# Sorted edge rows kept by step, lane and slot, and a second attention loop that loads them directly

## What is computed

```python
def _L2_gnn_ref(x, edge_attr, Wq, bq, Wk, bk, Wv, bv, We, be, bias, edge_index):
    H, C = 8, 32
    q = (x @ Wq + bq).reshape(n, H, C)
    k = (x @ Wk + bk).reshape(n, H, C)
    v = (x @ Wv + bv).reshape(n, H, C)
    dst = edge_index[0]
    src = edge_index[1]
    e = (edge_attr @ We + be).reshape(-1, H, C)
    key_j = k[src] + e
    alpha = (q[dst] * key_j).sum(-1) / math.sqrt(C)
    alpha = jax.nn.softmax(alpha, axis=0)
    out = v[src] * alpha[:, :, None]
    out = jax.ops.segment_sum(out, dst, num_segments=n)
    return out.reshape(n, H * C) + bias
# for each layer L of the four:
    h = jnp.maximum(_layernorm(x, axis=-1), 0.0)
    x = x + L(h, edge_index, ...)
```

## Time and profile before

| | |
|---|---|
| median of 3 runs | 4075.86 us (4073.83 to 4079.36) |
| span of the profiled execution | 4069.4 us |
| busy | PE 2803.7 (69%), DVE 2921.2 (72%), POOL 2699.3 (66%), ACT 942.5 (23%) |
| first attention loop, first to last step | 1675 to 2283 us |
| second attention loop, first to last step | 2519 to 3257 us |

### The profile page before, as it was taken

One profiled execution on the slowest core, in us unless ns is written; L12 is line 12 of the kernel. 1 busy time (PEld: TensorE's weight loads), 2 busy tenths in 40 slices (PEclk: granted clock), 3 DMA queues, 4 the chain that ended last, 5 costly groups with the idle time before them and its releaser, 6 DMA issues. The chain is left out here.

```text
span 4069.4 us, 59078 instructions
## 1 busy us (share of the span) xinstructions
PE 2803.7 (69%) x13465; PEld 1627.6 (40%) x13465; DVE 2921.2 (72%) x6759; ACT 942.5 (23%) x2732; POOL 2699.3 (66%) x2789
## 2 busy tenths in 40 slices
PE   5436779999997999699999876888888840000007
PEld 4335322222223887355555443555555530000004
DVE  7897458888885333599999774777777775666664
ACT  0020112222221332344444321222222220000004
POOL 0486667777664777677777475777777727777772
PEclk8555889999998999799999898999999975555558
DMA  4477357777765333577777433666666614444440
GB/s 173 151 237 269 88 156 208 205 202 201 206 195 134 63 68 70 157 211 212 211 208 207 100 83 102 191 191 189 191 190 191 186 40 109 108 108 108 108 105 33
DMA packets 418425, 627.24 MB, mean 154 GB/s; under 512 B 254045, under 2 KB 275650, under 8 KB 417296
## 3 DMA queue, kind: packets, MB, share of 16 engines
q0 software_dynamic: 173536, 520.88, 45.2%
q1 hardware_dynamic: 236336, 76.88, 8.0%
q10 hardware_dynamic: 8448, 28.18, 2.1%
HBM read 548.80 MB, written 76.56 MB: 154 GB/s over the span
## 5 line engine op out<-in xcount | busy, mean ns | idle before, releaser
L1219 POOL DMA_INDIRECT edge_ring<-tab,edge_rec x480 | 469.3, 978 | 199.7 <-issue 128.1
L2204 POOL DMA_INDIRECT state<-tab,edge_rec x480 | 453.9, 946 | 158.0 <-issue 145.9
L1843 PE MATMUL edge_psS<-edge_terms,ident 128*128 128x256 f32 x1952 | 471.5, 385 | 34.6 <-DVE edge_psS L1887 34.6
L1843 PEld LDWEIGHTS edge_psS<-edge_terms,ident 128*128 128x128 f32 x1952 | 369.1, 193 | 203.7 <-DVE edge_psS L1887 107.9
L2376 PE MATMUL gate_psT<-ident,gate_hb 128*128 128x128 f32 x50 | 10.0, 287 | 614.7 <-ACT gate_hb L2337 614.7
L1763 POOL DMA_INDIRECT state<-tab,edge_rec x360 | 340.4, 946 | 127.6 <-issue 104.5
L1281 PE MATMUL edge_psX<-state,ident 128*128 x720 | 377.7, 634 | 53.6 <-DVE edge_ring L1310 53.3
L1763 POOL DMA_INDIRECT state<-tab,edge_feat x360 | 340.4, 946 | 109.7 <-issue 104.8
L1862 PE MATMUL edge_psX<-state,ident 128*128 128x512 f32 x720 | 351.9, 612 | 84.5 <-DMA state<-tab,edge_feat 82.0
L1310 DVE TENSOR_TENSOR edge_ring<-edge_psX,edge_ring 128x1024 f32<-128x1024 f32 x240 | 293.9, 1225 | 97.2 <-PE edge_psX L1290 49.3
L1882 DVE TENSOR_TENSOR edge_terms<-state,edge_psW 128x1024 f32<-128x1024 f32 x180 | 219.8, 1221 | 116.9 <-ACT edge_psW L1820 110.5
(11 more groups left out here) (471 smaller groups left out, 6116.9 us busy)
## 6 DMA issues: line engine op xcount, KB each, us to landing
feat_d<-state SPq DMA_DIRECT2D x32, 528.0 KB, 5.1
sorted_d<-state SPq DMA_DIRECT2D x7, 2380.0 KB
edge_feat<-feat_d SPq DMA_DIRECT2D x113, 132.0 KB
state<-tab,edge_rec POOLq DMA_INDIRECT x840
state<-src_rows ACTq DMA_DIRECT2D x26, 512.0 KB
state<-low_rows ACTq DMA_DIRECT2D x26, 512.0 KB
edge_ring<-tab,edge_rec POOLq DMA_INDIRECT x600, 3.7
update_row_out<-in_edge_all SPq DMA_DIRECT2D x57, 128.0 KB
```

What stands on the lines that cost most here:

```text
L1219: pool.indirect_dma_start(out=ring[:, k, s, :], out_offset=None, in_=S["tab0"][:, :], in_offset=bass.IndirectOffsetOnAxis(ap=rec[:, k, R_S ...
L1843: last = pe.matmul(so_far, S["ident"][:, :], terms[:, s, :], start=False, stop=(s == QE - 1), skip_group_check=True)
L2204: pool.indirect_dma_start(out=ring[:, k, s, :], out_offset=None, in_=S["tab3"][:, :], in_offset=bass.IndirectOffsetOnAxis(ap=rec[:, k, R_S ...
```

## The change

Rows of `sorted_d` now lie by step (512 rows), within a step by lane, within a lane by slot, as long as there are at most NEAR_STEPS = 128 steps (`many` = 0 on the chip; with more steps `many` = 1, the rows lie as before and every step is gathered). So the rows of step k, all lanes, are one block of 512 rows, and SP can load it with one direct transfer.

- **attend(2):** SP's loop of near turns loads for each step the record and then the rows (`load_near`); POOL's loop has only the 4 gathers, which wait for `s_feat`. The last turn is a loop of its own: SP loads a record and then waits until POOL's gather of that step has landed (`pass_on`) before it goes to the next; POOL gathers three steps' rows first, then alternates. Near turns are all turns but one.
- **rank_edges:** the steps of the second order are prepared before the table `before` is made, since the place of a node now depends on the step at which its block begins (`apart`, `begins`, one more matmul); `before` counts in units of 128 rows, and a third matmul for each column of each look-up adds the lane (`lane_b`). The place is then taken apart into step, lane and slot (9 more instructions on 128 x 416), and the record turn has 3 more.
- **order_nodes:** the blank is 8 transfers of 68 rows a lane in place of 7 of 70 and a small one.

```diff
-BLANK_ROWS = 70
-SORTED_ROWS = -(-(QUADS + 1) * QE // (P * BLANK_ROWS)) * P * BLANK_ROWS
+STEP_ROWS = P * QE
+NEAR_STEPS = 128
+DUMP_ROW = (NEAR_STEPS + AQ) * STEP_ROWS
+SORTED_ROWS = 2 * NEAR_STEPS * STEP_ROWS
+BLANK_ROWS = DUMP_ROW // P // 8
...
+    def count_dve(self, dve, step, ps):
...
+        many, less, far = S["many"], self.less, self.far
+        step(dve.tensor_scalar(less[:, :], w[:, :], -1.0, None, ALU.add))
+        step(dve.tensor_scalar(far[:, :], less[:, :], many[:, 0:1], None, ALU.mult))
+        step(dve.tensor_scalar(S["far_turns1"][:, :], far[:, :], 1.0, None, ALU.add))
+        step(dve.tensor_tensor(less[:, :], less[:, :], far[:, :], ALU.subtract))
+        step(dve.tensor_copy(S["far_begin1"][:, :], less[:, :]))
+        step(dve.tensor_tensor(S["near_turns1"][:, :], less[:, :], many[:, :], ALU.add))
...
                     for j in range(COLS):
                         to = psL[h][:, j * NB:(j + 1) * NB]
                         pe.matmul(to, oh_lo[:, h, :, j], before[:, 0, :, t * COLS + j], start=True, stop=False)
-                        last = pe.matmul(to, oh_lo[:, h, :, j], before[:, 1, :, t * COLS + j], start=False, stop=True)
+                        pe.matmul(to, oh_lo[:, h, :, j], before[:, 1, :, t * COLS + j], start=False, stop=False)
+                        last = pe.matmul(to, oh_lo[:, h, :, j], lane_b[:, :], start=False, stop=True)
...
-                step(dve.tensor_scalar(first[:, :], cum[:, :], float(QE), None, ALU.mult))
+                halves(dve, step, node_i[:, :, :], node_l[:, :, :], (part[:, 0, :, :], part[:, 1, :, :], node_w[:, :, :]))
+                for a in range(2):
+                    dve.tensor_tensor(spread[:, a, :, :, :], ...).then_inc(s_spread, 1)
+                dve.wait_ge(s_by_lane, 1)
+                step(dve.tensor_copy(steps1.lanes[:, :, :], ...))
+                dve.nop().then_inc(s_lanes, 1)
+                steps1.prepare_dve(dve, step, psF, s_turned, s_most, s_at)
+                many = S["many"]
+                step(dve.tensor_scalar(steps1.apart[:, :], S["ident"][0:NB, 0:NB], steps1.scaled[:, 0:1], None, ALU.mult))
+                dve.nop().then_inc(s_apart, 1)
+                step(dve.tensor_scalar(many[:, :], psF[:, 3 * P + 1:3 * P + 2], float(NEAR_STEPS), None, ALU.is_gt))
+                step(dve.tensor_scalar(no_far[:, :], many[:, :], -1.0, 1.0, ALU.mult, ALU.add))
+                step(dve.tensor_scalar(lane_b[:, :], S["at_lane"][:, :], no_far[:, 0:1], None, ALU.mult))
+                dve.wait_ge(s_begins, 1)
+                step(dve.tensor_tensor(begins[:, :, :], S["in_block"][:, :, :], bc(psS[:, 3 * P:3 * P + NB], 1, [P, NB, NB]), ALU.mult))
+                step(dve.tensor_reduce(first[:, :], begins[:, :, :], AX.X, ALU.add))
+                step(dve.tensor_tensor(cum[:, :], cum[:, :], first[:, :], ALU.subtract))
+                step(dve.scalar_tensor_tensor(first[:, :], cum[:, :], many[:, 0:1], first[:, :], ALU.mult, ALU.add))
+                step(dve.tensor_scalar(first[:, :], first[:, :], float(STEP_ROWS), None, ALU.mult))
                 dve.nop().then_inc(s_first, 1)
+                steps1.count_dve(dve, step, psF)
+                dve.nop().then_inc(s_n1, 1)
...
-                step(dve.tensor_tensor(S["place_i"][:, :], place[:, :], above[:, :], ALU.add))
...
+                step(dve.tensor_tensor(to, place[:, :], above[:, :], ALU.add))
+                step(dve.tensor_scalar(near, to, P - 1, 2, ALU.bitwise_and, ALU.logical_shift_left))
+                step(dve.tensor_scalar(far, to, 7, QE - 1, ALU.logical_shift_right, ALU.bitwise_and))
+                step(dve.tensor_tensor(near, near, far, ALU.bitwise_or))
+                step(dve.tensor_scalar(far, to, 9, 9, ALU.logical_shift_right, ALU.logical_shift_left))
+                step(dve.tensor_tensor(near, near, far, ALU.bitwise_or))
+                step(dve.tensor_scalar(far, to, 7, None, ALU.logical_shift_right))
+                step(dve.tensor_scalar(near, near, no_far[:, 0:1], None, ALU.mult))
+                step(dve.tensor_scalar(far, far, many[:, 0:1], None, ALU.mult))
+                step(dve.tensor_tensor(to, near, far, ALU.add))
...
+                def load_near(q, at):
+                    sp.dma_start(feat[:, q % RING, :, :].rearrange("p s f -> p (s f)"),
+                                 steps_of[:, bass.ds(at, 1), :].rearrange("p a f -> p (a f)")).then_inc(s_feat[q % RING], 16)
+
+                def pass_on(t, q):
+                    hold(sp, s_far[q % RING], uses(t, q, RING) * 16)
+                    sp.nop().then_inc(s_feat[q % RING], 16)
...
+                    steps_of = S["sorted_d"].rearrange("(c p r) f -> p c (r f)", p=P, r=QE)
+                    m, near, begin = near_turns(sp), near_begin(sp), far_begin(sp)
+                    with nc.Fori(0, m, engines=[sp.engine], hint_back_edge=True) as t:
+                        for q in range(AQ):
+                            load(t, q, t * AQ + q)
+                            load_near(q, (t + near) * AQ + q)
+                    with nc.Fori(0, far_turns(sp), engines=[sp.engine], hint_back_edge=True) as t:
+                        for q in range(AQ):
+                            load(t + m, q, (t + begin) * AQ + q)
+                            pass_on(t, q)
...
-                def rows(t, q):
-                    k = q % RING
...
-                        hold(pool, s_rec[(q + TURNED) % RING], uses(t, q + TURNED, RING) * 16)
-                        features((q + TURNED) % RING)
-                        hold(pool, s_feat[k], uses(t, q, RING) * 16)
...
+                    m = near_turns(pool)
+                    with nc.Fori(0, m, engines=[pool.engine], hint_back_edge=True) as t:
+                        for q in range(AQ):
+                            hold(pool, s_feat[q % RING], uses(t, q, RING) * 16)
+                            rows(q % RING)
+                    with nc.Fori(0, far_turns(pool), engines=[pool.engine], hint_back_edge=True) as t:
+                        for q in range(AQ):
+                            if q == 0:
+                                for a in range(TURNED):
+                                    far_features(t, t + m, a)
+                            if q + TURNED < AQ:
+                                far_features(t, t + m, q + TURNED)
+                            hold(pool, s_feat[q % RING], uses(t + m, q, RING) * 16)
+                            rows(q % RING)
```

More of the change, by code:

```diff
@@ L212, in __init__ @@
         self.n = sb("n", [P, 1], I32)
+        if i == 1:
+            self.less, self.far = sb("less", [P, 1]), sb("far", [P, 1])
+            self.apart = sb("apart", [NB, NB])
     def prepare_pe(self, pe, ps, s_lanes, s_turned, s_most, s_at):
@@ L399, in _ @@
                 steps.prepare_dve(dve, step, turned, s_turned, s_most, s_at)
+                steps.count_dve(dve, step, turned)
             @block.tensor
@@ L478, in rank_edges @@
         first = ph.sb("first", [P, NB])
+        begins = ph.sb("begins", [P, NB, NB])
+        lane_b = ph.sb("lane_b", [P, NB], BF16)
+        no_far = ph.sb("no_far", [P, 1])
         w0 = ph.sb("w0", [P, NB])
@@ L534, in rank_edges @@
         cols = lambda t: slice(t * COLS, (t + 1) * COLS)
-        CH, CH1 = 19, 8
+        CH, CH1 = 19, 11
         with nc.Block() as block:
@@ L620, in _ @@
                 pe.matmul(psS[:, 64:64 + NB], S["ones"][:, :], node_w[:, :, 1], start=True, stop=True).then_inc(s_pre, 1)
+                for a in range(2):
+                    pe.wait_ge(s_spread, a + 1)
+                    last = to_lanes(pe, S, psS[:, 2 * P:2 * P + 2 * NB], spread, a)
+                last.then_inc(s_by_lane, 1)
+                pe.wait_ge(s_lanes, 1)
+                steps1.prepare_pe(pe, psF, s_lanes, s_turned, s_most, s_at)
+                pe.wait_ge(s_apart, 1)
+                pe.matmul(psS[:, 3 * P:3 * P + NB], S["ones"][0:NB, :], steps1.apart[:, :], start=True, stop=True).then_inc(s_begins, 1)
                 pe.wait_ge(s_bf, 1)
@@ L634, in _ @@
                     look_up(t)
-                    if t == 1:
-                        for a in range(2):
-                            pe.wait_ge(s_spread, a + 1)
-                            last = to_lanes(pe, S, psS[:, 2 * P:2 * P + 2 * NB], spread, a)
-                        last.then_inc(s_by_lane, 1)
                 n = steps0.turns(pe)
@@ L761, in _ @@
                 dve.nop().then_inc(s_bf, 1)
-                halves(dve, step, node_i[:, :, :], node_l[:, :, :], (part[:, 0, :, :], part[:, 1, :, :], node_w[:, :, :]))
-                for a in range(2):
-                    dve.tensor_tensor(spread[:, a, :, :, :], bc(S["in_block"][:, :, :], 3, [P, NB, NB, 2]), bc(part[:, a, :, :], 2, [P, NB, NB, 2]), ALU.mult).then_inc(s_spread, 1)
                 def low(t):
@@ L907, in shared @@
     sb("far_turns", [P, 1], I32)
+    for n in ("near_turns1", "far_turns1", "near_begin1", "far_begin1"):
+        sb(n, [P, 1], I32)
     sb("adst", [P, NB])
@@ L1729, in load @@
```

(9 more changed lines are left out.)

104 lines of the change are left out of this document (62 added, 42 removed).

## The result

| | before | after |
|---|---|---|
| median | 4074.85 us (4070.41 to 4079.36, 4 runs) | 3979.2 us (3972.42 to 3980.32, 4 runs) |
| span of the profiled execution | 4069.4 us | 3976.9 us |
| loop 1, first to last step | 608.4 us | 605.5 us |
| loop 2, first to last step | 737.6 us | 636.5 us |

The ratio of the changed kernel to the one before is 0.9761, with a 95% interval of 0.9747 to 0.9775. The forecast was 3973 us with a range of 3954 to 4004. The span fell by 92.5 us where the sum said 103. The median came nearer to the forecast than the span did, since it lies 2.3 us over the profiled span here and the forecast had added 6.5.

The account below looks back on a forecast made before the run. The prediction took POOL's gather issue to bound loop 2, with PE next. Loop 2 -113.6, its start and end -3.7 and rank_edges +14.3 summed to -103, a span of 3966 and a median of 3973 us, range 3954 to 4004.

Parts of the forecast that it names:

- What bounds the loop: Loop 2: POOL's descriptor work bounds it at 50.0 us a turn; after the change PE does, at 41.7.
- the rival of a lock between PE and DVE: Attention loop 2: PE and DVE wait on each other, adding at most 3 us a turn, 4015 us; chance 0.12.
- The boundary of a turn: Loop 2, between turns: PE stalls where DVE pauses, taken at 1.1 us, between 0 and 1.8.
- The last turn: Loop 2's gathered turn: 23 us extra on POOL, about 20 covered by its lead, so 3 come through (0 to 15).
- then 5 gathers a step: Last turn of loop 2, behind its head: five gathers in place of four, (6.25 - 5.07) x 7 = 8 us extra.
- the cover: Head of loop 2's last turn: POOL's lead from eight ring buffers, some 6 PE steps, hides about 20 us.
- Start and end: Loop 2: first table gather 2.7 us earlier (1 to 4), and 1 us less at the end; 3.7 together.
- rank_edges: The phase that places rows: new preparation, third matmul, place and record-turn instructions cost +14.3 us in sum (8 to 26).
- The third matmul: rank_edges look-ups: 14 behind the loads of rows pay 0.3 us each, +4 us (0 to 15).
- The place instructions: rank_edges: three more products of 128 x 416 and six integer shifts, 4.3 us with gaps.
- Cost nothing: Larger blank writes, scatters to other rows and the record DMA's companion on SP's queue were to add no time.
- The rival in which POOL sets the pace: Loop 2: PE hides its boundary stall, POOL paces turns at 40.0 us but has no lead, 3962 us; chance 0.13.

Follow-up runs that it names:

- 36-gather kernel: Changed kernel plus one extra gather of sorted rows on POOL in every second near step, into an unread buffer: 4033.48 us, 0.9893 of before.
- the layout alone: Changed kernel with the second loop as before, gathering sorted rows in every step: 4089.19 us, 1.0020 of before.
- The kernel with two transposes: Changed kernel with two transposes and one ACT copy per layer-2 step in place of four and two, for timing only: 3969.54 us, 0.9731 of before.
- the records ahead: Changed kernel whose last turn loads the record of step q+2 before SP waits for the gather of step q: 3969.47 us, 0.9728 of before.
- the lane in `first`: Changed kernel with the lane added once to `first` instead of by the third matmul: 3979.38 us; also with last-turn records taken two steps ahead: 3968.91 us.
- the one that gathers all turns: Changed kernel with the bound of 128 steps set to 0, so 15 turns gather their rows: 4334.42 us, 1.0640 of before.

## Why the prediction was right, point by point

- **What bounds the loop.** POOL's issue before, PE after: right. The 36-gather kernel puts the turn at POOL's 45.0, the layout alone leaves it at 50.0, and fewer transposes shorten it. The PE step of 5.07 us was measured to the hundredth, and PE goes from step to step in it without a wait, so the rival of a lock between PE and DVE is out too.
- **The boundary of a turn.** Taken at 1.1 us, measured 42.0 - 40.6 = 1.4. With the first turn at 43.7, the near turns took 589.7 us, where 14 x 41.7 + 2 is 585.8: 4 us of the miss. The kernel with two transposes shows what the term hangs on: the less PE leads DVE's work, the more of DVE's pause of 1.8 us it pays.
- **The last turn.** The mechanism was named (three serial rounds at the head, then a gather more per step) and mis-sized: 3 us were to come through, 11.4 did. Two terms failed. The first is "then 5 gathers a step", priced at POOL's 6.25. The serial round doesn't end with the head: each later gather of rows still waits for a record that SP fetches only after the one before has landed, and from 3102.63 to 3139.77 us five of them took 7.4 us each. These five steps put POOL 11.8 us further behind PE, where 8 were priced for all seven. The larger miss is the cover. POOL was ready for the last turn at 3091.26 us, and PE came to the table rows of its first step at 3112.21:

```profile
3112.21 1.88 PE L1953 MATMUL edge_psX<-state,ident 128*128 128x512 f32 x4
...
3118.33 1.99 PE L1953 MATMUL edge_psX<-state,ident 128*128 128x512 f32 x4 [0.89 <-DMA state<-tab,edge_feat]
```

  That is 21.0 us, of which a step's four gathers and their landing take 7.4 (from POOL's first one for the next step at 3110.96 to PE's start at 3118.33, where PE waited for them). So the cover was 13.6 us and not 20, and the head alone, 12.6 us from 3091.26 to 3103.88 (15 were priced), used nearly all of it. 12.6 + 11.8 - 13.6 = 10.8 of the 11.4. Why the cover was short: I gave every ring slot some 6 steps, but the last slot is reloaded later than the others, since its record is needed until the sum of the next turn's first step is written. SP's timeline shows the gap:

```profile
3071.41 0.33 SPq L1789 DMA_DIRECT2D edge_rec<-rec_d  x1
...
3081.08 0.33 SPq L1789 DMA_DIRECT2D edge_rec<-rec_d  x1
```

  9.7 us where the reloads before it are 5 apart, and every turn has this gap. The slot before it is reloaded 31 us ahead of PE's use, the last one 26. So POOL stood still for 3.4 us just ahead of the last turn, and its lead there was some 5 us shorter than I had it (argued from this gap, not tested by itself). With the records ahead, what is left of both costs nothing.
- **Start and end.** The start gained 2.9 us between SP's first record and POOL's first table gather, forecast 2.7: right. The 1 us at the end isn't there: from the last step of loop 2 to the end of the span it is 812.6 us in both traces.
- **A figure of the Trainium skill.** For a DMA that GpSimd issues, the Trainium skill ("DMA: Bandwidth & Descriptors", section "Anatomy of one DMA — SWDGE (gpsimd) path") gives about 2.0 us plus its bytes over 436 GB/s. Carried over to the direct load of 139 KB, which SyncE issues and for which the page doesn't give it, that is an estimate of 2.3 us. In the changed kernel's trace this load took 2.8 at the least and 3.6 in the middle:

```profile
DMA to landing us min/median/max: 2.8/3.6/4.2
```

  The gather of the same bytes, which POOL does issue, took 2.8 and 3.2. So the trace agrees with the estimate in neither, and the rows of the record and of the gather, 2.9 and 3.2, were the better guide.
- **rank_edges.** Forecast +14.3, measured +9.9 between the two profiled executions, +9.8 between the means of two traces before and nine with this phase as changed. The first look-up came 12.4 us later (the kernel before, then the changed one):

```profile
308.88 0.93 DVE L780 TENSOR_TENSOR state<-rank_psL,rank_oh_hi 128x400 f32<-128x400 f32 x1 [1.05 <-PE rank_psL L631]
...
321.29 0.93 DVE L824 TENSOR_TENSOR state<-rank_psL,rank_oh_hi 128x400 f32<-128x400 f32 x1 [1.96 <-PE rank_psL L664]
```

  5.0 of that is the preparation, which only moved, so the new work cost 7.4 for 7.9. But the record turn came only 7.3 us later: 5.1 were slack, where 2.8 were taken. The wait for POOL at L708 is gone (0.20 us are left of 2.81, and of 5.50 in the second trace of the kernel before), as forecast, and the rest went into waits of the first twelve look-ups for loads of rows. The third matmul was over-priced, 4 us for some 2: the look-ups behind the record turn grew by 2.2, 1.0 of it in the last period and 0.1 in each of the others, not 0.3. The place instructions cost what the sum said, 4.4 us from L851 to L859 for 4.3, and the three of the record turn 1.0 for 0.9.
- **Cost nothing.** Not quite. From the end of rank_edges to the first step of loop 1 two traces before have 1251.6 and 1251.8 us; the changed kernel has 1255.7 and 1256.0. That is 4 us that the sum didn't have. Three microseconds of it came back in the first two turns of loop 1 in the first trace, but not in the second. The two kernels with the lane in `first` have 1251.9 and 1253.3, the one that gathers all turns 1252.3, and other traces with the changed layout up to 1259. Whether it is where the rows are scattered or chance between executions stays open.
- **The ledger of the two profiled executions.** rank_edges +9.9, the phases up to loop 1 +4.1, loop 1 -2.9, up to loop 2 -2.6, loop 2 -101.1, the rest 0: together -92.5, with rounding. So the forecast was helped by misses that cancel in part: loop 2 gave 12.5 us less than summed and the 4.1 us up to loop 1 weren't in the sum, while rank_edges cost 4.4 less.
- **Slips in the sums.** Half of each end gives 3962 to 3990, not 3958 to 3992. The rival in which POOL sets the pace at 40.0 us a turn goes against the sum's own 40.6 for PE's eight steps; measured, POOL waits 1.9 us a turn on average and PE sets the pace. The record's 2.9 us is over both loops; in loop 2 alone it was 2.3, and 3.3 in the changed kernel's.

## What to carry to other kernels

When the engine that issues gathers is the bound, count issues: one gather of rows cost 1.25 us of POOL however it landed, and moving it to an idle queue as a direct transfer took each turn down to the next engine's time, and no further. Check the cover of the last turn as carefully as the pace of the others. A loop that is taken only once can cost as much as a quarter of its own length where it puts a load, a gather and a landing in series; take the small loads ahead of the wait. Price a lead in a ring by the slot that comes free last (here argued, not tested by itself).

## What the runs showed of the hardware

A gather took POOL 1.25 us (0.95 and 0.30 of "issue") whether it fetched 1088 B of sorted rows or 2 KB of a table row for each lane, in both kernels.

The busy share of the DMA engines didn't scale with the bytes: 23% more bytes per step, in direct transfers of 139 KB, raised it from 0.78 to 0.88 and the throughput from 226 to 278 GB/s, with not a tenth of a microsecond per turn lost. In the kernel that gathered more in every second step the share was 0.78 at 223 GB/s. So in this mix a share near 0.8 was not yet the engines' limit.
